# Score tiles of one key tile by 512 queries, a bank per head, with the low part of the keys on half of the rows for each head

## The reference

```python
q = (X @ Wq)  # 16 heads of 64;  k, v = X @ Wk, X @ Wv  # 8 heads of 64, each serves two query heads
q, k = rope(q), rope(k)
att = einsum('bhqd,bhkd->bhqk', q, k) * 256**-0.5
att = 50 * tanh(att / 50)
att = softmax(where(causal, att, -inf))
x = layernorm(X + (att @ v) @ Wo)
x = layernorm(x + int8_linear(per_token_quant(x)))   # 512 by 512, result in float16
```

## Time and profile before

| | |
|---|---|
| median of 3 runs | 1495.42 us (1493.2 to 1499.96) |
| the profiled execution | 1498.59 us |
| its span, first to last instruction | 1496.8 us |
| TensorE busy | 1327.0 us, 89% of the span |
| VectorE busy | 1094.6 us, 73% |
| ScalarE busy | 847.4 us, 57% |
| GpSimd busy | 379.1 us, 25% |
| mean granted TensorE clock | 0.939 of full speed |

### The profile page before, as it was taken

How to read it: one execution, slowest core, us unless ns; L and a number is a source line. 1 busy time by engine, 2 the same in 40 slices (tenths; PEclk the granted TensorE clock), 3 DMA queues, 4 the chain that set the end, 5 groups by cost and what they waited for, 6 DMA issues and landing times.

```text
span 1496.8 us, 17694 instructions
## 1 busy us (share of the span) xinstructions
PE 1327.0 (89%) x5824; PEld 964.5 (64%) x5840; DVE 1094.6 (73%) x1367; ACT 847.4 (57%) x952; POOL 379.1 (25%) x448
## 2 busy tenths in 40 slices
PE   6479999888987999998987999989799799999794
PEld 5356777666665777675755677767576577776462
DVE  4368888782687788885477788878357788888485
ACT  4156777761236777864232877676223486779332
POOL 2231111111462111110265112111136311111275
PEclk9889999998998999999899899999899899999896
DMA  7755445474424345537341444445642244343431
GB/s 281 259 194 153 114 112 133 115 213 158 129 61 105 92 115 133 165 84 222 127 140 50 109 118 124 107 146 149 207 136 79 79 115 107 99 108 105 152 108 42
DMA packets 117038, 196.23 MB, mean 131 GB/s; under 512 B 28498, under 2 KB 70484, under 8 KB 112724
## 3 DMA queue, kind: packets, MB, share of 16 engines
q1 hardware_dynamic: 112340, 186.73, 44.1%
q10 hardware_dynamic: 4608, 8.39, 1.5%
HBM read 89.39 MB, written 38.54 MB: 85 GB/s over the span
## 4 chain that ended last, share of the span: by engine, by line
PE 55%; SPq 14%; DVE 11%; DMA 7%; issue 6%; ACT 3%; POOL 3%; DVEq 0%; ACTq 0%; POOLq 0%
PE ps L720 18%; PE ps L694 13%; PE ps L643 13%; SPq L474 8%; PE ps L757 6%; PE ps L665 4%; SPq L487 3%; DMA d_scratch<-sums 2%; DMA rows<-r_scratch 2%; SPq L465 1%; DMA qk<-work_r 1%; ACT probs L888 1%; DVE probs L1138 1%; DVE stats L1159 1%; SPq L490 1%
## 5 line engine op out<-in xcount | busy, mean ns | idle before, releaser
L720 PE MATMUL ps<-prob_hi,v 128*65 128x512 f32 (+3 forms) x1280 | 415.0, 374 | 5.9 <-DVE prob_lo L1077 5.9
L694 PE MATMUL ps<-qk 128*128 128x512 f32 (+1 forms) x1280 | 326.8, 382 | 71.7 <-DMA qk<-work_r 40.3
L888 ACT ACTIVATE probs<-ps 128x1024 f32<-128x1024 f32 x288 | 293.4, 1019 | 148.6 <-PE ps L694 147.2
L1077 DVE TENSOR_TENSOR prob_lo<-probs,prob_hi 128x1024 fp32r<-128x1024 f32 x288 | 355.6, 1235 | 9.9
L1286 POOL TENSOR_SCALAR_AFFINE_SELECT probs<-probs 128x256 f32<-128x256 f32 (+1 forms) x192 | 144.7, 761 | 805.4 <-ACT probs L893 805.4
L694 PEld LDWEIGHTS ps<-qk 128*128 128x128 f32 x1280 | 230.4, 194 | 137.6 <-issue 39.7
L893 ACT ACTIVATE probs<-probs 128x1024 f32<-128x1024 f32 x288 | 305.7, 1061 | 8.8
L1073 DVE CAST prob_hi<-probs 128x1024 fp32r<-128x1024 f32 x288 | 205.9, 715 | 128.4 <-POOL probs L1286 80.1
L643 PE MATMUL ps<-xT,w_ring 128*128 128x512 f32 x1152 | 291.2, 398 | 1.6 <-DVE v L1022 1.5
L643 PEld LDWEIGHTS ps<-xT,w_ring 128*128 128x128 f32 x1152 | 218.9, 192 | 48.5 <-issue 2.2
L720 PE MATMUL ps<-prob_lo,v 128*65 128x512 f32 (+1 forms) x640 | 238.8, 373 | 0.0
(11 more groups left out here) (77 smaller groups left out, 1041.7 us busy)
## 6 DMA issues: line engine op xcount, KB each, us to landing
qk<-work_r SPq DMA_DIRECT2D x256, 128.0 KB, 2.3
qk<-work_r SPq DMA_DIRECT2D x512, 64.0 KB, 2.0
y_scratch<-sums SPq DMA_DIRECT2D x256, 64.0 KB
wo<-wo_scratch SPq DMA_DIRECT2D x8, 2048.0 KB, 8.0
y_raw<-y_scratch SPq DMA_DIRECT2D x32, 512.0 KB, 3.6
w_ring<-w_scratch SPq DMA_DIRECT2D x15, 1024.0 KB, 5.3
x_raw<-X_T SPq DMA_DIRECT2D x16, 512.0 KB, 5.8
x_in<-X SPq DMA_DIRECT2D x32, 256.0 KB, 2.8
```

What stands on the lines that cost most here:

```text
L694: mm = nc.tensor.matmul(scores[:, g % 2, col:col + REP * w].rearrange("p (h q) -> p h q", h=REP), qk[:, n % 2, i, 2 + part, keys], qk[:, n ...
L720: mm = nc.tensor.matmul(sums_ps[:, :, GQ - w:GQ], v[:, kt, v0:v0 + width], p[:, g % ring, col:col + REP * w].rearrange("p (h q) -> p h q", ...
L888: nc.scalar.activation(probs[:, g % PRING, :], scores[:, g % 2, :], ACT.Tanh, scale=SCORE_SCALE / SOFTCAP).then_inc(capped, 1)
L1077: nc.vector.tensor_tensor(prob_lo[:, g % PRING, :], probs[:, g % PRING, :], prob_hi[:, g % HRING, :].bitcast(F32), ALU.subtract).then_inc( ...
```

## The change

The two banks of a score tile are now one bank for each query head. A tile has segments, one key tile by up to 512 queries, and `segments(s)` lists them as (key tile, first query, width, column). Five of the nine tiles have one segment of 512, two have 256 and 256, two have 384 and 128. The columns in a tile and the number of tiles stay.

The high keys are multiplied by high and low queries over all 128 rows, with one matmul per segment and head. The low keys are multiplied by the high queries alone, over 64 rows: head 0 on rows 0 to 63, head 1 on rows 64 to 127. For this the queries of head 1 lie the other way round, high part on the upper rows (`r0` in `put`). The product of low by low is no longer formed. A tile has 4 or 8 score matmuls (1664 in all, 1280 before), first all on 128 rows, then all on 64.

`strips(s)` cuts the segments at the borders of the query groups for `weigh`, 20 strips over 9 tiles as before. Group 0 now ends at tile 1 (before: 0), group 1 at tile 2 (2), group 2 at tile 7 (5), group 3 at tile 8 (8). Groups 2 and 3 start at tiles 2 and 3 (before: 2 and 5). The masks are one for each diagonal block, with both heads: 8 over 9 tiles (before: 6).

```diff
+    def segments(s):
+        rows = {0: [(0, 0, HT)], 1: [(1, P, 3 * P), (3, 3 * P, P)], 2: [(2, 2 * P, GQ), (4, HT, GQ)],
+                7: [(5, 5 * P, 3 * P), (7, 7 * P, P)], 8: [(4, 6 * P, GQ), (6, 6 * P, GQ)]}.get(s, [(s - 3, HT, HT)])
+        cols = itertools.accumulate([0] + [w for _, _, w in rows[:-1]])
+        return [(*row, col) for row, col in zip(rows, cols)]
...
     def strips(s):
         found = []
-        for i in range(2):
-            for n, (c, kt) in enumerate(SCORE_BANKS[2 * s + i]):
-                late = kt == 2 * c + 1
-                found.append((c, kt, i * 512 + n * GQ, c * GQ + late * P, P if late else GQ))
+        for kt, q0, w, col in segments(s):
+            for c in range(q0 // GQ, (q0 + w - 1) // GQ + 1):
+                lo, hi = max(q0, c * GQ), min(q0 + w, (c + 1) * GQ)
+                found.append((c, kt, col + lo - q0, hi - lo))
         return found
...
-                                r0 = 64 * low + 32 * half
+                                r0 = 64 * (low ^ r) + 32 * half
...
-                for c, kt, col, q0, w in strips(s):
-                    keys = slice(kt * P, (kt + 1) * P)
-                    for part in (0, 1):
-                        mm = nc.tensor.matmul(
-                            scores[:, g % 2, col:col + REP * w].rearrange("p (h q) -> p h q", h=REP),
-                            qk[:, n % 2, i, 2 + part, keys], qk[:, n % 2, i, 0:REP, q0:q0 + w],
-                            start=(part == 0), stop=(part == 1))
+                out = scores[:, g % 2, :].rearrange("p (h q) -> p h q", h=REP)
+                for h in range(REP):
+                    for kt, q0, w, col in segments(s):
+                        nc.tensor.matmul(out[:, h, col:col + w], qk[:, n % 2, i, 2, kt * P:(kt + 1) * P],
+                                         qk[:, n % 2, i, h, q0:q0 + w], start=(col == 0), stop=False,
+                                         skip_group_check=True)
+                for kt, q0, w, col in segments(s):
+                    for h in range(REP):
+                        half = slice(h * HD, (h + 1) * HD)
+                        mm = nc.tensor.matmul(out[:, h, col:col + w], qk[half, n % 2, i, 3, kt * P:(kt + 1) * P],
+                                              qk[half, n % 2, i, h, q0:q0 + w], start=False, stop=True,
+                                              skip_group_check=True)
                 mm.then_inc(scored, 1)
...
-                    first = (c, kt) == ((c, 0) if c % 2 == 0 else (c, 2 * c + 1))
+                    first = kt == (4 if c == 2 else 0)
...
-                            p[:, g % ring, col:col + REP * w].rearrange("p (h q) -> p h q", h=REP),
+                            p[:, g % ring, :].rearrange("p (h q) -> p h q", h=REP)[:, :, col:col + w],
...
-                for col, n, step in diagonals(g % NS):
+                for col in diagonals(g % NS):
                     view = probs[:, g % PRING, col:col + P]
                     diag = bass.AP(tensor=view.tensor, offset=view.offset,
-                                   ap=[[PRING * T, P], [step, n], [1, P]])
+                                   ap=[[PRING * T, P], [HT, REP], [1, P]])
```

More of the change, by code:

```diff
@@ L1 @@
+import itertools
 from contextlib import ExitStack
@@ L58, in attention_block @@
     assert (T, C, REP, HD, KC, NT) == (1024, 512, 2, 64, 4, 8)
-    def whole(c):
-        return [[(c, kt)] for kt in range(2 * c + 1)]
-    SCORE_BANKS = whole(0) + [[(0, 1), (1, 3)]] + whole(1) + whole(2) + [[(2, 5), (3, 7)]] + whole(3)
-    NS = len(SCORE_BANKS) // 2
+    def segments(s):
[3 more added lines that the diff above has]
+        return [(*row, col) for row, col in zip(rows, cols)]
+    NS = 9
     NB = NKV * NS
@@ L69, in strips @@
         found = []
-        for i in range(2):
-            for n, (c, kt) in enumerate(SCORE_BANKS[2 * s + i]):
-                late = kt == 2 * c + 1
-                found.append((c, kt, i * 512 + n * GQ, c * GQ + late * P, P if late else GQ))
+        for kt, q0, w, col in segments(s):
+            for c in range(q0 // GQ, (q0 + w - 1) // GQ + 1):
+                lo, hi = max(q0, c * GQ), min(q0 + w, (c + 1) * GQ)
+                found.append((c, kt, col + lo - q0, hi - lo))
         return found
     def diagonals(s):
-        found = []
-        for i in range(2):
-            for n, (c, kt) in enumerate(SCORE_BANKS[2 * s + i]):
-                if kt == 2 * c:
-                    found.append((i * 512, 2, GQ))
-                elif kt == 2 * c + 1 and n == 0:
-                    found.append((i * 512, 4, P))
-        return found
+        return [col for kt, q0, w, col in segments(s) if q0 == kt * P]
     LAST_TILE = [max(s for s in range(NS) if any(f[0] == c for f in strips(s))) for c in range(G)]
@@ L705, in weigh @@
                     pe.wait_ge(ones_set, 1)
-                for c, kt, col, q0, w in strips(s):
-                    first = (c, kt) == ((c, 0) if c % 2 == 0 else (c, 2 * c + 1))
+                for c, kt, col, w in strips(s):
+                    first = kt == (4 if c == 2 else 0)
                     if first and (j, c) == (0, 0) and b >= 1:
@@ L1281, in mask @@
                 pool.sem_inc(wait_passed, 1)
-                for col, n, step in diagonals(g % NS):
+                for col in diagonals(g % NS):
                     view = probs[:, g % PRING, col:col + P]
                     diag = bass.AP(tensor=view.tensor, offset=view.offset,
-                                   ap=[[PRING * T, P], [step, n], [1, P]])
+                                   ap=[[PRING * T, P], [HT, REP], [1, P]])
                     nc.gpsimd.affine_select(out=diag, in_=diag, compare_op=ALU.is_ge, fill=0.0, base=0,
-                                            pattern=[[0, n], [1, P]], channel_multiplier=-1
+                                            pattern=[[0, REP], [1, P]], channel_multiplier=-1
                                             ).then_inc(masked, 1)
```

## The result

The changed kernel takes 1559.99 us (median of 4 runs, 1556.99 to 1564.46), the kernel before beside it 1494.31 (1493.2 to 1499.96). The ratio is 1.0434, with a 95% interval of 1.0396 to 1.0472: 4.3% slower, 65.7 us. The forecast was 1572, the range 1518 to 1610. The profiled execution has a span of 1562.7 us (before: 1496.8) and a mean granted clock of 0.931.

A forecast was written before the change was run, and what follows sets the result against it. The prediction took TensorE as the bound, full in middle units. Added TensorE time 95, hidden -21, group order +2 and late put +1 made +77 us on the 1495.4 median: 1572 us, 8-in-10 range 1518 to 1610.

The forecast's parts named there:

- TensorE's term: Scores of all 288 tiles: +0.33 us a tile in the mean, +95 us of TensorE time.
- The price of a switch: TensorE's two row-mode changes per score tile: 0.20 us each, a pause and then a load that nothing hides.
- The second half starts 0.107 after the first: Low-key matmul pairs: 128-column loads follow no closer than 0.11 us, so the second half starts 0.107 us later.
- The 66 us that the prediction named: Alternative estimate of the sum, near +66 us, if the low halves start about 4 ns apart as the skill page says.
- The score part: First high matmul to next full one: 1.20, 1.30 or 1.34 us by segment kind, against 0.92 before.
- Hidden: Added TensorE time vanishing in existing waits: 7.5 and 5 us in fourth units, 6 and 2.5 in first units; -21 together.
- The order of the groups: TensorE waiting for ScalarE's copy of the sums at query group 3: 0.3 us in each of 8 units, +2 us.
- The put at the end: Last batch's end: group 2 completes later, so its put (line 487) is late, about +1 us.
- the masks: Masks go from 6 to 8 per 9 tiles, 64 more of 0.74 us on GpSimd, which has waiting time: nothing.
- Serial halves: Rival: the low halves don't overlap, the second starts after the first; 34 us more, 1604 us; chance 0.13.
- A cheap switch: Rival: a row-mode switch costs only its bare load, 0.11 us; +32 us, 1527 us; chance 0.12.
- No switch: Rival: halves need no row-mode switch, so the kernel gets faster, 1476 us between 1465 and 1487; chance 0.11.

The follow-up runs named there:

- The extra pairs of the experiment: The changed kernel with each segment's low matmuls right behind its high ones, two more row-mode switches in each of 128 two-segment tiles: 1600.17 us, ratio 1.0688.
- the first experiment: The changed kernel with its low-key matmuls over all 128 rows for both heads, so without any switch of row mode: 1542.52 us, ratio 1.0312.

## Why the prediction was right, and where its terms were off

The side and the mechanism were right, the time was 12 us too high (65.7 measured, 77 forecast), and that closeness is luck: TensorE's term was 49 us too large, and the other three, -18 us together, came to about +20, 38 too small. Of the signs that the prediction named, the 0.32 us ahead of the low load came; the 0.11 between the low starts didn't; and long waits of TensorE for the copy of the sums did come, 16.8 us, the sign that the order costs more than 2 us.

- **The price of a switch (0.20 us).** Right for the entry: 0.32 us from the last high matmul to the low load, 0.09 beyond the 0.23 of its columns, and 0.107 for the bare load. The extra pairs of the experiment cost 0.40. For the exit it depends on what comes next: with a projection (128 columns) 0.20, with a weighing (65 columns) 0.10 + 0.055 = 0.155. I took line 735's neighbours, all of 128 columns, as the price of every exit.
- **The second half starts 0.107 after the first.** This was the term of the sum that was wrong. The halves start together; with both on the same rows the pair takes 0.22 us more. I took a floor read from loads over all rows for one over halves, and kept it although no row showed two halves. The Trainium skill, page "TensorE: Matmul & The Clock Gate", Part 3, The mechanism, was the better guide: it has tiles on different row groups start about 4 ns apart, and here most stand 3 or 4 ns apart. The 66 us that the prediction named beside it as an estimate is not confirmed by that, since the TensorE sum measured 46.
- **The score part.** 1.04 us with one segment (forecast 1.20), 1.05 with 256 and 256 (1.30), 1.10 with 384 and 128 (1.34), before a weighing. TensorE's sum is 46 us, not 95. The floor for 128 columns holds over all rows (1.09 us a tile in the first experiment), but with halves it costs 0.05.
- **Hidden (-21 us).** In the first units of batches 1 to 3 it was right in kind: 2.0 to 2.5 us of growth where TensorE has 2.9 more and the copy 0.6 on top. The first unit of all hid nothing. In the fourth units I let 5 us lie beside SP's unbroken puts and 7.5 ahead of them, and there the sign was wrong: those stretches grew by 22.4 us, beyond the TensorE work of a unit (2.9 each). The runs of the new order without the low part, with more switches, with serial halves and with the low part over all rows take 582.6, 584.3, 583.4 and 583.9 us there against 585.9, the old order with halves 559.9. So TensorE's work is hidden there altogether, and the growth belongs to the new order and its queue. The last unit, where the forecast hid nothing of its 6 us, grew by 0.8 only (from its first score matmul to the end of its last, 42.3 to 43.1): ScalarE, busy for 39 us of it before, probably holds its pace; no run tested that.
- **The order of the groups (+2 us).** The wait in step 15 was rightly named and sized at 0.3 us a unit against 0.6. What was missed is what the earlier groups do to the queue. Their stores come right behind 2 MB loads and are waited for twice: by the next copy on ScalarE (7.6 us to land, TensorE idle 2.76) and by SP at line 407 (5.9 idle). The later load of the reciprocals returned 15.5 us of it, the earlier copy perhaps 4 more. What then remains, 1540, is near the old order's 1536.5. Read from that side, the halves with their switches cost 41 to 44 us and the order 20 to 23; read from the first experiment, the order costs 46 and the halves 17. The stretches give an estimate between the two: 22.4 us from the fourth units' starts to the next batch, 5 in step 15 of the middle units (8 times 0.6) and 5 in the first unit of all (73.1 against the old order's 68.2) are the order's, 32 together, and the other 34 are the halves'. The first unit of all waits for a late store too. Its copy in step 15 needs one that SP issues only behind 16 puts, at 144.66, though it then lands within 1.8 us.
- **The put at the end (+1) and the masks (nothing).** From the last unit's start to the end it is 1.0 us longer, of which 0.7 lie ahead of the end of the last weighing: at most 0.3 are left for the put's delay. The masks are 583 ns each and not 739, and GpSimd is idle before them for 857 us.
- **The rivals.** "Serial halves" is settled by its own run: it was 1605.77, against 1604 worked out, but isn't what happens. (Its 0.19 for the tiles with 384 and 128 columns is 0.13 by the prediction's own terms, which makes 30 us of the 34.) "A cheap switch" (0.11) is excluded by the 0.40 of a pair. "No switch" fails with it; without any low part at all the order gives only 1.7%, so the 1476 of that rival was about the best that this order and queue allow.

One thing stays open: the split between the halves and the order is an estimate, since either costs less when the other is there, and no run has the new order without any of its waits. Of the experiments that moved single loads only the first brought time back; the others moved a wait elsewhere. What the lower clock behind the longer waits costs in all was read in one place only.

## What to carry to other kernels

Count the changes of row mode before the columns: a pair cost 0.36 to 0.40 us of TensorE here, over one and a half matmuls of 512 columns, so by these numbers work on half the rows can pay only where several matmuls share one change (here 0.23 us were saved for at least 0.36). When the order of tiles changes, follow every store and load that is tied to the end of a group through its queue, since a wait for the landing of a small store is cheap only while no large transfer is ahead of it. Moving the large one away helped here only where nothing urgent stood behind its new place.

## What the runs showed of the hardware

- Two matmuls over 64 rows each, on different halves of the rows and into different banks, start 3 or 4 ns apart, at most 10, and hide each other completely; their loads do too (0.19 us for two, as for one). On the same rows a pair of 512 columns takes 0.22 us more.
- A change from 128 rows to 64 or back costs a pause of about 0.10 us and then a bare load, which takes as long as it has columns: 0.107 for 128, 0.055 for 65. A change to 4 rows and back cost as much before loads of 128 columns (0.32 us from the last matmul to the next load, both ways).
- A small store of sums took 1.8 us to land, and 6 to 7.6 us with a 2 MB load ahead of it on the same queue; it landed 0.4 to 0.8 us after that load.
